# A gated MLP sandwich in fp32: the transposes of h moved from TensorE to VectorE blocks and DMAs

## What is computed

```
x = x + layernorm(attn(layernorm(x)))
x = x + layernorm(ffn(layernorm(x)))

attn(x): s = silu(x @ w_gate.T)                 # (tokens, 1376)
         per token, the 688 smallest |s| are set to 0 (top_k of -|s|)
         return (s * (x @ w_up.T)) @ w_down.T
ffn(x):  return (silu(x @ W_gate.T) * (x @ W_up.T)) @ W_down.T
```

## Time and profile before

| | us |
|---|---|
| median of 3 runs | 786.71 (786.11 to 787.39) |
| the profiled execution | 787.0 |
| its span | 785.0 |
| PE busy | 766.9 (98%) |
| VectorE busy | 406.5 (52%) |
| ScalarE busy | 346.5 (44%) |
| GpSimd busy | 117.8 (15%) |
| packets of the DMA queue, their share of 16 engines | 22288, 19.3% |

### The profile page before, as it was taken

One profiled execution on the slowest core, in us unless ns is written; L12 is line 12 of the kernel. 1 busy time (PEld: TensorE's weight loads), 2 busy tenths in 40 slices (PEclk: granted clock), 3 DMA queues, 4 the chain that ended last, 5 costly groups with the idle time before them and its releaser, 6 DMA issues.

```text
span 785.0 us, 9833 instructions
## 1 busy us (share of the span) xinstructions
PE 766.9 (98%) x3593; PEld 646.2 (82%) x3593; DVE 406.5 (52%) x822; ACT 346.5 (44%) x575; POOL 117.8 (15%) x278
## 2 busy tenths in 40 slices
PE   8999999999999999999989999999999999999996
PEld 7888888888888888889877788788878888788884
DVE  7686766766667666785783443253224332151114
ACT  6787665656656666566843221131112111131112
POOL 0533321122211222212310000010001000010001
PEclk9999999999999999999999999999999999999999
DMA  8520102222022220223713101020010210021001
GB/s 288 165 74 28 45 32 77 77 77 76 2 77 77 76 91 28 77 78 103 276 43 137 59 15 40 1 94 15 13 41 28 67 41 1 0 93 42 0 1 54
DMA packets 22338, 51.18 MB, mean 65 GB/s; under 512 B 2320, under 2 KB 5904, under 8 KB 22096
## 3 DMA queue, kind: packets, MB, share of 16 engines
q1 hardware_dynamic: 22288, 50.54, 19.3%
HBM read 42.14 MB, written 16.84 MB: 75 GB/s over the span
## 4 chain that ended last, share of the span: by engine, by line
PE 83%; DVE 7%; ACT 3%; issue 3%; POOL 2%; DMA 1%; DVEq 0%; POOLq 0%; SPq 0%; ACTq 0%
PE gu_ps L468 29%; PE gu_ps L418 23%; PE y_ps L447 13%; PE tr_ps L489 11%; PE y_ps L489 4%; PE tr_ps L432 2%; ACT junk L617 1%; PE tr_ps L400 1%; DMA xin<-in_L_attn_x 1%; PE gu_ps L400 1%; DVE below L973 1%; POOL thr L1224 1%; POOL move L1221 1%; DVE gate_lo L846 1%; DVE up_lo L858 0%
## 5 line engine op out<-in xcount | busy, mean ns | idle before, releaser
L617 ACT ACTIVATE junk<-absv,thr 128x1383 bf16<-128x1383 f32 x96 | 139.3, 1451 | 57.9 <-POOL thr L1224 56.4
L1023 DVE TENSOR_TENSOR prod<-gu_ps,prod 128x512 f32<-128x512 f32 (+1 forms) x44 | 30.4, 690 | 182.9 <-PE gu_ps L468 182.9
L418 PE MATMUL gu_ps<-up_hi,xT 128*128 128x460 f32 (+1 forms) x384 | 111.3, 371 | 0.0
L418 PE MATMUL gu_ps<-gate_hi,xT 128*128 128x460 f32 (+1 forms) x384 | 111.1, 370 | 0.0
L447 PE MATMUL y_ps<-down_hi,hT 128*128 128x512 f32 (+1 forms) x352 | 110.3, 395 | 0.0
L673 ACT ACTIVATE prod<-gu_ps 128x512 f32<-128x512 f32 (+1 forms) x44 | 26.3, 597 | 127.4 <-PE gu_ps L468 127.4
L447 PEld LDWEIGHTS y_ps<-down_hi,hT 128*128 128x128 f32 (+1 forms) x352 | 66.9, 190 | 15.0
L418 PEld LDWEIGHTS gu_ps<-gate_hi,xT 128*128 128x128 f32 x384 | 72.2, 188 | 7.8
L418 PEld LDWEIGHTS gu_ps<-up_hi,xT 128*128 128x128 f32 x384 | 72.2, 188 | 7.7
L447 PE MATMUL y_ps<-down_lo,hT 128*128 128x512 f32 (+1 forms) x176 | 70.3, 399 | 4.5 <-DVE hT L892 4.4
L418 PE MATMUL gu_ps<-up_lo,xT 128*128 128x460 f32 (+1 forms) x192 | 73.2, 381 | 1.5 <-DVE up_lo L846 0.8
(11 more groups left out here) (115 smaller groups left out, 1370.3 us busy)
## 6 DMA issues: line engine op xcount, KB each, us to landing
xin<-x_scratch SPq DMA_DIRECT2D x18, 256.0 KB, 3.2
xin<-in_L_attn_x SPq DMA_DIRECT2D x16, 256.0 KB, 4.6
xres<-in_L_attn_x SPq DMA_DIRECT2D x16, 256.0 KB, 4.8
x_scratch<-xres SPq DMA_DIRECT2D x16, 256.0 KB, 2.0
xres<-x_scratch SPq DMA_DIRECT2D x14, 256.0 KB, 2.8
out<-xres SPq DMA_DIRECT2D x14, 256.0 KB, 2.1
raw<-in_L_ffn_W_gate SPq DMA_DIRECT2D x4, 688.0 KB, 4.9
raw<-in_L_ffn_W_up SPq DMA_DIRECT2D x4, 688.0 KB, 4.7
```

Source lines behind the costliest of these rows:

```text
L418: last = nc.tensor.matmul(dst[:, 0:CW[n]], xt, w, start=(c == 0 and i == 0), stop=(c == KC - 1 and i == 2))
L617: nc.scalar.activation(junk[:, 0:I + PAD], absv[:, q, 0:I + PAD], ACT.Sign, bias=thr[:, q:q + 1], scale=-1.0, accum_out=sgn[:, q:q + 1]).t ...
L1023: nc.vector.tensor_tensor(prod[0:k, 0, GW:2 * GW], bank(("u", idx, 0))[0:k, :], prod[0:k, 0, 0:GW], ALU.mult).then_inc(p2_done, 1)
```

## The change

For tiles 2 to 13 (`H_MOVED`) the transposes of h leave TensorE. VectorE transposes `prod[:, j % 2]` in place (`swap_h`): each 32x32 block is turned, and a block stays where it was. SP then carries the blocks to their partitions (`move_h`): 16 DMAs per tile, one for each pair of a partition quarter q of the source and e of the destination, each with 32 partitions and 11 (for e = 3, 10) runs of 32 floats, from `prod` into `hT[:, 1]`. `split_h_hi` and `split_h_lo` read `hT[:, 1]` instead of PSUM, the low half in place. `silu(j, n)` waits for the landing of all 16 DMAs of tile j-2 instead of the transposes. Tiles 0, 1, 14 and 15 are as before. The same is written for x (`X_MOVED`), but it is empty: no tile of x is moved.

The order changes too: on TensorE the down product and x's transposes come after up 0 instead of before it (steps 4 to 14); on VectorE `x_stats` comes before `find_flag` and `select`, and `swap_h(j - 1)` after `x_normalise`; on GpSimd `x_rstd` comes before the first `newton`; on SP `move_h(j - 1)` comes after the loads and before the store, and in the second block some x loads are reordered.

```diff
+    H_MOVED = range(2, TILES - 2)
+    X_MOVED = ()
+    H_TURN = {j: k for k, j in enumerate(j for j in range(TILES) if j not in H_MOVED)}
+    H_MOVE = {j: k for k, j in enumerate(H_MOVED)}
...
+    BLK = 32
+    BLOCKS = [(q, e) for q in range(4) for e in range(4)]
...
+            def move_h(j):
+                if j not in H_MOVE:
+                    return
+                sp.wait_ge(hswap_done, H_MOVE[j] + 1)
+                sp.wait_ge(y_done, j)
+                raw_h = hT[:, 1, :].rearrange("p (c t) -> p c t", c=JC)
+                src = prod[:, j % 2, :].rearrange("p (c e t) -> p c e t", c=JC, e=4)
+                for q, e in BLOCKS:
+                    n = JC if e < 3 else JC - 1
+                    sp.dma_start(raw_h[e * BLK:(e + 1) * BLK, 0:n, q * BLK:(q + 1) * BLK].bitcast(F32),
+                                 src[q * BLK:(q + 1) * BLK, 0:n, e, :]).then_inc(h_moved, 16)
...
                 if j in TWO:
                     load_x(XSEQ[POS[j + 1] + 2])
+                if j >= 3:
+                    move_h(j - 1)
+                    move_x(XSEQ[POS[j + 1] + 1])
                 store(j - 2)
...
             def transpose_h(j):
 
+                if j in H_MOVE:
+                    return
...
                 product(j, 0, 2)
-                down(j - 2)
-                transpose_x(j + 1)
+                if j - 2 not in H_MOVE:
+                    down(j - 2)
+                    transpose_x(j + 1)
                 product(j, 1, 0)
+                if j - 2 in H_MOVE:
+                    down(j - 2)
+                    transpose_x(j + 1)
                 product(j, 1, 1)
...
             def silu(j, n):
                 act.wait_ge(g_done, G_AT[j, n])
-                if j >= 2:
-                    act.wait_ge(h_tr, 3 * (j - 2) + n + 1)
+                if j - 2 in H_TURN:
+                    act.wait_ge(h_tr, 3 * H_TURN[j - 2] + n + 1)
+                elif j >= 2:
+                    act.wait_ge(h_moved, 256 * (H_MOVE[j - 2] + 1))
...
+            def swap_h(j):
+                if j in H_MOVE:
+                    dve.wait_ge(h_done, j + 1)
+                    nc.vector.transpose(prod[:, j % 2, :], prod[:, j % 2, :]).then_inc(hswap_done, 1)
...
                     split_h_lo(j - 2)
                     abs_values(j)
+                x_stats(a[1])
                 find_flag(j - 1)
                 select(j - 1)
-                x_stats(a[1])
                 x_normalise(a[1])
+                swap_h(j - 1)
                 split_x_lo(j + 1)
...
                 units(j)
+                x_rstd(XSEQ[p + 1])
                 newton(j, 0)
-                if j > 3:
-                    x_rstd(XSEQ[p + 1])
                 newton(j, 1)
                 newton(j, 2)
```

More of the change, by code:

```diff
@@ L82, in sandwich @@
     HALF = H // 2
+    H_MOVED = range(2, TILES - 2)
+    X_MOVED = ()
+    H_TURN = {j: k for k, j in enumerate(j for j in range(TILES) if j not in H_MOVED)}
+    H_MOVE = {j: k for k, j in enumerate(H_MOVED)}
+    X_TURN = {a: k for k, a in enumerate(a for p, a in enumerate(XSEQ) if p not in X_MOVED)}
+    X_MOVE = {a: k for k, a in enumerate(a for p, a in enumerate(XSEQ) if p in X_MOVED)}
+    BLK = 32
+    BLOCKS = [(q, e) for q in range(4) for e in range(4)]
     def width(j):
@@ L205, in sandwich @@
         half_done = sem("half_done")
+        xswap_done, hswap_done, h_moved = map(sem, ("xswap_done", "hswap_done", "h_moved"))
+        x_moved = [sem(f"x_moved{i}") for i in range(2)]
         exact = sem("exact")
@@ L222, in sandwich @@
                 ring += [("g", g * JC + j, 0), ("u", g * JC + j, 0)]
-                if j in X_AT and g < GROUPS - 1:
+                if j in X_AT and g < GROUPS - 1 and TILES + GT * (g + 1) + X_AT[j] in X_TURN:
                     ring.append(("X", TILES + GT * (g + 1) + X_AT[j], 0))
@@ L234, in x_bank, with x_place @@
             return tr_ps[1] if a == 1 else tr_ps[2]
+        def x_place(a):
+            if a < TILES:
+                return (xT[:, a % 2, s, :].rearrange("p (c t) -> p c t", c=KC) for s in range(2))
+            g, r = divmod(a - TILES, GT)
+            return (x_group(g)[:, s, :, r * P:(r + 1) * P] for s in range(2))
         @block.sync
@@ L244, in load_x @@
                 if p >= 2:
-                    sp.wait_ge(x_tr, p - 1)
+                    before = XSEQ[p - 2]
+                    if before in X_TURN:
+                        sp.wait_ge(x_tr, X_TURN[before] + 1)
+                    else:
+                        sp.wait_ge(x_moved[X_MOVE[before] % 2], 256 * (X_MOVE[before] // 2 + 1))
                 if a >= TILES:
@@ L249, in load_x, with move_x @@
                 sp.dma_start(xin[:, p % 2, :], src).then_inc(x_in[p % 2], 16)
+            def move_x(a):
+                if a not in X_MOVE:
+                    return
+                sp.wait_ge(xswap_done, X_MOVE[a] + 1)
+                if a < TILES:
+                    sp.wait_ge(u_done, U_AT[a - 2, 2])
+                elif a < TILES + GT:
+                    sp.wait_ge(wlo_done, NP)
+                elif a < TILES + 2 * GT:
+                    sp.wait_ge(h_done, TILES)
+                else:
+                    sp.wait_ge(u2_done, ((a - TILES) // GT - 1) * JC)
+                _, raw_x = x_place(a)
+                src = xin[:, POS[a] % 2, :].rearrange("p (c e t) -> p c e t", c=KC, e=4)
+                for q, e in BLOCKS:
+                    sp.dma_start(raw_x[e * BLK:(e + 1) * BLK, :, q * BLK:(q + 1) * BLK].bitcast(F32),
+                                 src[q * BLK:(q + 1) * BLK, :, e, :]).then_inc(x_moved[X_MOVE[a] % 2], 16)
+            def move_h(j):
[5 more added lines that the diff above has]
+                src = prod[:, j % 2, :].rearrange("p (c e t) -> p c e t", c=JC, e=4)
+                for q, e in BLOCKS:
+                    n = JC if e < 3 else JC - 1
+                    sp.dma_start(raw_h[e * BLK:(e + 1) * BLK, 0:n, q * BLK:(q + 1) * BLK].bitcast(F32),
+                                 src[q * BLK:(q + 1) * BLK, 0:n, e, :]).then_inc(h_moved, 16)
             def load_w(w):
@@ L333, in _ @@
                     load_x(XSEQ[POS[j + 1] + 2])
+                if j >= 3:
+                    move_h(j - 1)
+                    move_x(XSEQ[POS[j + 1] + 1])
                 store(j - 2)
+                if j in TWO and XSEQ[POS[j + 1] + 2] < TILES + GT:
+                    move_x(XSEQ[POS[j + 1] + 2])
                 if j >= 3:
@@ L358, in _ @@
                     if g < GROUPS - 1:
+                        move_x(b + 4)
                         load_x(b + 6)
[L360 to L363, removed]
+                if g < GROUPS - 1:
+                    move_x(b + 5)
+                    load_x(b + 7)
+                    move_x(b + 6)
+                    if g < GROUPS - 2:
+                        load_x(b + 8)
+                    move_x(b + 7)
+                    if g < GROUPS - 2:
+                        load_x(b + 9)
                 load_res(b)
@@ L632, in split_x_hi @@
             def split_x_hi(a):
[L633 to L636, removed]
-                        act.wait_ge(u_done, U_AT[a - 2, 2])
[L638 to L645, removed]
+                hi, raw_x = x_place(a)
+                if a in X_MOVE:
+                    act.wait_ge(x_moved[X_MOVE[a] % 2], 256 * (X_MOVE[a] // 2 + 1))
+                    src = raw_x.bitcast(F32)
+                else:
+                    act.wait_ge(x_tr, X_TURN[a] + 1)
+                    src = x_bank(a)[:, :].rearrange("p (c t) -> p c t", c=KC)
+                    if 2 <= a < TILES:
+                        act.wait_ge(u_done, U_AT[a - 2, 2])
+                    elif a >= TILES + 2 * GT:
+                        act.wait_ge(u2_done, ((a - TILES) // GT - 1) * JC)
+                nc.scalar.activation(hi, src, ACT.Copy).then_inc(xhi_done, 1)
             def split_h_hi(j):
+                if j in H_MOVE:
+                    act.wait_ge(h_moved, 256 * (H_MOVE[j] + 1))
                 for g, (c0, cn) in enumerate(TG):
[L649 to L653, removed]
+                    cols = slice(c0 * P, (c0 + cn) * P)
+                    if j in H_MOVE:
+                        src = hT[:, 1, cols].bitcast(F32)
+                    else:
+                        act.wait_ge(h_tr, 3 * H_TURN[j] + g + 1)
+                        if g == 0 and j >= 1:
+                            act.wait_ge(y_done, j)
+                        src = tr_ps[g][:, 0:cn * P]
+                    nc.scalar.activation(hT[:, 0, cols], src, ACT.Copy).then_inc(hhi_done, 1)
             def normalise_y(b):
```

24 lines of the change are left out of this document (14 added, 10 removed).

## The result

| | before | after |
|---|---|---|
| median, side by side | 786.49 (4 runs, 786.11 to 787.39) | 795.88 (4 runs, 794.92 to 796.03) |
| ratio, 95% interval | | 1.0115 [1.0098, 1.0133] |
| profiled span | 785.0 | 793.8 |

The changed kernel is 9.4 us slower. The forecast was 772.3; the time lies in the range (769.5 to 806), on the other side of no change. The page of the changed kernel: busy times, the DMA queue, the shares of the chain.

A forecast was written before the change was run, and what follows sets the result against it. PE was taken as the bound, 24.30 us a step. Removing 12 x 1.20 = 14.4 us from span 785.0 gives 770.6; with 2.0 outside the span and 0.3 less for the median, 772.3. Range 769.5 to 806.

The forecast's parts named there:

- 772.3 + 11 x (D - 10.6): Time if a tile's move lasts D over 10.6 us: forecast time plus the excess in each of 11 loop periods.
- the limit: Longest move, 10.6 us, whose landing still lets silu 2 start when PE's gate product 2 ends, 7.59 into the step.
- the issue price: On SP, 16 DMA issues per tile: 5.9 us at the least, 7.5 at 0.47 each; plus 2.3 landing, D = 9.8.
- the rival: Rival 2: DMA engines or SP's issues become the bound, above 27 ns per packet or 0.6 us per issue; slower; chance 0.31.
- break-even of D = 11.9: Move length at which the loop's loss equals the 14.4 us gained: 1.3 us over 10.6, times 11.
- lower end of 7.9: Least length claimed for a tile's move, in us, against the 9.8 taken for the forecast.
- It fits: On SP: x load issued at 26.2 lands near 8 of the next step; statistics want it at 9.8.
- rival 3: Block boundary: late weight copy delays the pair loads 2 to 4 us, or late x load delays select; 774 to 777; chance 0.11.
- a move at 17.8 of its step: Move's start: VectorE's transpose ends at about 17.8 us, the down product at 17.65, counted from the first gate product.
- the step of 23.1: PE's step without the 11 transposes of h: 15.10 + 7.59 + 0.44 = 23.1 us, before 24.30.
- the loop's period, 12.5 + D: Loop of landing, silu 0 to 2 (2.3), silu 2 to VectorE transpose's end (10.2), and move D, against PE's 23.1 us.
- the low side: DMA packets of 128 B priced by bytes, 6 ns each, 2 us per tile, instead of 84 ns, 29 us per tile.

The follow-up runs named there:

- the run that takes it out: In steps 4 to 9 the next step's x load is issued ahead of the 16 DMAs on SP, otherwise the changed kernel; 794.38 us.
- SP's twelve and ScalarE's four: Changed kernel with 12 of each move's 16 DMAs issued by SP and 4 by ScalarE, all of h carried; 775.41 us.

## Why the prediction was wrong, and where it was right

The runs on the scale of the prediction. D is measured in each trace, from the end of the swap to the landing of the last DMA, over the moves of tiles 2 to 12, which the formula's eleven periods hold. The formula is the prediction's.

| DMAs on SP | issue, landing (us) | D, least to most | mean D | 772.3 + 11 x (D - 10.6), not below 772.3 | measured |
|---|---|---|---|---|---|
| 8 | 0.62, 2.1 | 6.7 to 7.8 | 7.3 | 772.3 | 771.45 |
| 12 | 0.62, 2.1 | 9.4 to 10.7 | 9.8 | 772.3 | 772.21 |
| 14 | 0.62, 2.1 | 10.7 to 12.0 | 11.08 | 777.6 | 781.59 |
| 16, one run a partition | 0.591, 1.9 | 11.3 to 12.3 | 11.62 | 783.5 | 788.2 |
| 16, 160 pieces | 0.603, 1.9 | 11.6 to 12.6 | 11.88 | 786.4 | 793.0 |
| 16, as changed | 0.617, 2.1 | 12.0 to 13.0 | 12.29 | 790.9 | 795.88 |

The order is right and the place of the limit too, but once the loop is closed the kernels are 4 to 7 us slower than the formula: the length of the move alone does not make up the loss.

**The term that failed is the issue price**, "16 of them: 5.9 us at the least, 7.5 at 0.47 each". It is 0.617 with 0.04 between, and the whole row takes 10.5 to 11.6 us. The prediction's D also counts one issue too many, because the landing is counted from the start of the last issue: its own sum is 15 x 0.47 + 2.3 = 9.35, and with the measured price it is 15 x 0.657 + 2.1 = 12.0, which is the least that the trace shows. The 0.47 is the 0.43 of the residual load, plus 0.04. Rows that were at hand said more. In the same timeline the weight copy right behind the store takes 0.49, and the x load behind both 0.58:

```profile
239.93 0.58 SPq L249 DMA_DIRECT2D xin<-in_L_attn_x  x1
```

And the six loads of the earlier trace rows start between 423.3 and 426.3, which is 0.60 from one to the next, the price at which the rival begins. For a DMA between partitions the row is not even needed: the first of each 16, behind a queue that had mostly been idle for some 12 us, takes 0.61 to 0.62 (0.73 the very first time), against 0.33 for a plain one behind an idle queue. So no row of the kernel before held this price, and the two bounds of 0.33 and 0.47 came from another kind of DMA. The rival was priced at "0.6 us per issue" and that is what happened. Its break-even of D = 11.9 was too generous: the kernel with a D of 11.6 measures 1.9 us slower than before. With a limit of 10.6 and a lower end of 7.9, an upper end for the issue belonged in the sum: the rows showed 0.98 in a row of six, which by itself gives D = 18. The chance of 0.31 was too low where an error of 0.13 us, sixteen times over, changes the sign; it was 0.19 (0.657 for 0.47).

**The second failed step is "It fits"** for the x load. It was to land near 8 of the step; behind 10.5 to 11.6 us of issues it lands at 257.28, and that step's first gate product started at 247.28 - 2 x 2.516 = 242.25: 15.0 of the step. It holds select through the statistics. It followed from the same term, and is worth about 1.9 us here (the period less D, 12.67 against 12.50 in the run that takes it out).

**The third part of the loss was the boundary**, rival 3, which I had set beside the slow rival and not on top of it. In SP's timeline the last weight copy now goes out behind the last move (376.37) and lands at 381.72, and the pair loads wait for it (before: gate pairs issued at 370.51, up pairs at 377.99, 7.5 us apart):

```profile
376.37 0.55 SPq L324 DMA_DIRECT2D raw<-in_L_ffn_W_down  x1
...
381.74 2.98 SPq L334 DMA_DIRECT2D gate_lo<-raw  x6
385.21 2.80 SPq L334 DMA_DIRECT2D up_lo<-raw  x6
```

The chain of waits then leads from the last products of PE through the first of the up pairs; before, it went through ScalarE's counts there:

```profile
367.62 17.57 PE gu_ps L485 x84
385.21 8.70 DMA up_lo<-raw
```

The gate pairs go out 3.5 us before the up pairs and no longer 7.5, and from down 13 to down 14 it takes 19.2 us instead of 16.7. Formula (790.9), x load (1.9) and boundary (2.4) together are 795.2, and 795.88 was measured. So near a sum is in part luck, for it leaves out a fourth part. The first swap ends only 11.6 us ahead of the down product that PE could start (in the kernel with eight DMAs; 15.7 in a later step there), so the first moved tile already makes PE late, by 2.5 us, where the prediction starts the loop from a move at 17.8 of its step. Against the kernel with twelve DMAs, by the starts of the down products: 2.4 us up to tile 2, 19.0 from 2 to 12, 3.4 from 12 to 15. With twelve DMAs 13 to 14 takes 16.74, so the boundary rival needs the long move as well.

**What held.** 1.20 us of transposes a tile and the step of 23.1 (23.07 in four kernels); the swap (1.64 for 1.65); the landing (2.1 for 2.3); the limit of 10.6 (a mean D of 9.8 is free, 11.1 costs); the loop's period, 12.5 + D: swap ends follow each other by (365.1 - 90.5) / 11 = 24.96 us, and 12.5 + 12.3 is 24.8, the rest being the x load's; the DMA engines are not the bound, with the low side taken from rows far off. Per packet the difference of the two profiles gives (0.260 x 793.8 - 0.193 x 785.0) x 16 / (91408 - 22288) = 12.7 ns, twice the 6 ns by bytes, so a part that does not go with the bytes does show, and below the 20 ns at which the engines would have fallen behind. The warning of the Trainium skill, "DMA: Bandwidth & Descriptors", Specifications (read-modify-write below 512 B), did not become the bound: the engines were 0.39 busy during a move. What its section "Why small descriptors are slow (HBM only)" exempts agrees with the run of long pieces in the main: they gained 0.7 us a tile and no more. The trace agrees with its rule that transfers under 64 KB are mostly overhead, with the overhead at a place that I had not put it: 0.6 us of the issuing queue for each 45 KB.

Half held: the 2.5 us that ScalarE's counts were to gain from the earlier reciprocal root. The count that waited 2.58 us waits 0.56, but the next one waits 1.91, for a reason in the last section.

## What to carry to other kernels

When a change puts a row of DMAs into one queue, price the row as issues in series: 0.65 us each here, with any pieces that were tried, plus one landing counted from the start of the last, and then ask which loop of waits has that row in it and how much room that loop has. If the room is short of n issues, take away DMAs or put some on a second issuing engine that has time at that point, before anything is done to layouts; and look at what stands behind the row in the queue, which pays the same delay. If an unknown price times its count crosses the break-even inside its own bounds, the chances must lie close to even.

## What the runs showed of the hardware

**The issue.** A DMA between partitions takes 0.59 to 0.62 us of its queue with 32, 160 or 352 pieces, and 0.64 on ScalarE, against 0.33 for a lone plain one. With 160 or 352 pieces the first of a row, behind an idle queue, pays the same 0.61; with 32 it takes 0.51. A plain store, 0.33 when alone, takes 0.60 right behind such a row. The engine that issues decides it: SP's twelve and ScalarE's four ran at full pace at once.

Long issues of 1.0 to 2.0 us turn up two or three times in twelve moves. All 25 that the traces of the moving kernels show on SP start within 0.7 us of a packet of the queue that the profile calls q8 instruction, as here beside the issue of 1.67 at 244.14 (window 243.8 to 245.8):

```profile
q8 instruction: 1, 0.02, 4.4%
```

In the changed kernel three such packets fall into a row of 16, and these are the three long issues; in seven other kernels one more such packet falls beside an issue of ordinary length. That the packet makes the issue long is not shown by a run of its own.

**VectorE and GpSimd.** The count with the wait of 1.91 us stands behind a GpSimd operation on one column that takes 1.59 us in place of 0.31. GpSimd's timeline, and VectorE's instruction at the same time:

```profile
233.62 0.31 POOL L1309 TENSOR_SCALAR move<-sgn 128x1 f32<-128x1 f32 x1
...
236.04 1.59 POOL L1309 TENSOR_SCALAR move<-sgn 128x1 f32<-128x1 f32 x1 [1.67 <-ACT junk L690]
```

```profile
235.83 1.65 DVE L1100 SCALAR_TENSOR_TENSOR prod<-absv,kth,prod 128x1376 f32<-128x1376 f32 x1 [0.88 <-DVE anyflag L1091]
```

The move ends as select does. The new order has brought the newton steps under VectorE's select: the run of the order alone, without any move, shows the same (1.50 us at 229.24, beside a select from 228.9). Over the whole run the group's mean is 534 ns there, 530 here and 364 before:

```profile
L1309 POOL TENSOR_SCALAR move<-sgn 128x1 f32<-128x1 f32 x80 | 42.4, 530 | 86.8 <-ACT junk L690 86.4
```

The Trainium skill, "SBUF — State Buffer", SBUF: two separate sides, says that a VectorE operation with two SBUF inputs and a GpSimd operation that reads SBUF hold a shared port in turns, each for its whole instruction; the trace agrees, 1.59 us beside a select of 1.65. No run here takes the port away from one of the two, so the cause is the page's and not shown.
